# Count stage of a sparse attention kernel: first spreads moved ahead of the branch, projections spread over all counting rounds, query bias added by TensorE, mask kept as 0/1

## The reference, cut to what matters

```python
idx = prior_indices[:Ss]                     # 1024 queries x 32 keys, all key numbers under 256
Q, K, V = (proj(Wq, bq), proj(Wk, bk), proj(Wv, bv))   # x @ W.T + b, 2 batches, 16 heads of 16
s_scores = jnp.einsum('bhsd,bhskd->bhsk', Q, K[:, :, idx]) * scale
s_scores = jnp.where(prior_index_mask, s_scores, -inf)
sparse_out = jnp.einsum('bhsk,bhskd->bhsd', softmax(s_scores), V[:, :, idx])
...
out = sparse_out @ Wo.T + bo                 # if lam >= 1 for the batch, else a dense attention
x = x + ffn0(out)                            # a dense two-layer network
x = x + experts(cond1(x))                    # a second network, 8 experts, the best 2
```

## Time and profile before

| | |
|---|---|
| median of 3 runs | 575.02 us (574.04 to 575.03) |
| the profiled execution, its own time | 575.06 us |
| its span in the trace | 573.0 us |
| TensorE (PE) busy | 523.4 us, 91% of the span |
| VectorE (DVE) busy | 407.1 us, 71% |
| ScalarE (ACT) busy | 225.8 us, 39% |
| GpSimd (POOL) busy | 84.2 us, 15% |
| HBM | 26 GB/s over the span |

### The profile page before, as it was taken

The page is one execution under the profiler, slowest core; times in us unless marked ns, Lnnn a source line. Parts: engine busy times, 40 slices in busy tenths (PEclk is TensorE's granted clock), DMA queues, the critical chain, the costliest instruction groups (busy, mean ns, idle before and its releaser), DMA issues.

```text
span 573.0 us, 7404 instructions
## 1 busy us (share of the span) xinstructions
PE 523.4 (91%) x2649; PEld 361.9 (63%) x2649; DVE 407.1 (71%) x788; ACT 225.8 (39%) x381; POOL 84.2 (15%) x94
## 2 busy tenths in 40 slices
PE   3897788999899999989779999999999999999897
PEld 1454354454454454435557887888878888788786
DVE  5887879969896878734666588483884838848286
ACT  4204376667566576664345250032500325003100
POOL 3002643315123121200131100010000100000000
PEclk9998899999999999989879999999999999999989
DMA  6100010101010000000252000100001000010000
GB/s 248 56 2 1 0 38 37 38 1 38 1 37 1 1 0 2 3 0 1 80 146 73 1 2 18 47 9 0 2 19 46 11 0 2 18 47 0 11 9 27
DMA packets 11757, 15.38 MB, mean 27 GB/s; under 512 B 5954, under 2 KB 8258, under 8 KB 11714
## 3 DMA queue, kind: packets, MB, share of 16 engines
q1 hardware_dynamic: 11714, 14.83, 8.1%
HBM read 12.73 MB, written 2.10 MB: 26 GB/s over the span
## 4 chain that ended last, share of the span: by engine, by line
PE 72%; DVE 13%; ACT 8%; issue 3%; POOL 2%; DMA 1%; SPq 0%; ACTq 0%; DVEq 0%; POOLq 0%
PE psS L524 6%; PE psO L540 5%; PE psG L1544 4%; PE psG L1546 4%; PE psG L1545 4%; PE psM L1544 3%; PE psM L1546 3%; PE psM L1545 3%; PE psO L1544 3%; PE psO L1545 3%; PE psO L1546 3%; PE psG L504 3%; PE psS L1544 3%; PE psG L506 3%; PE psS L1546 3%
## 5 line engine op out<-in xcount | busy, mean ns | idle before, releaser
L737 DVE TENSOR_REDUCE few_Qa<-psG 128x2 fp32r<-128x512 f32 x116 | 74.6, 686 | 29.6 <-PE psG L506 29.5
L657 ACT ACTIVATE Pr<-psS 128x512 f32<-128x512 f32 x128 | 71.5, 599 | 30.1 <-PE psS L528 21.1
L744 DVE SCALAR_TENSOR_TENSOR Pr<-Pr,few_W 128x1024 f32<-128x1024 f32 x48 | 72.8, 1519 | 11.8 <-ACT Pr L657 11.6
L524 PE MATMUL psS<-few_QAT,few_KP 128*128 128x512 f32 x128 | 53.2, 460 | 10.5 <-ACT Pr L657 9.8
L504 PE MATMUL psG<-few_KG,QG 128*128 128x512 f32 x116 | 52.3, 508 | 3.7 <-DVE few_Qa L737 3.7
L1654 ACT ACTIVATE V<-psS,cols 128x512 f32<-128x512 f32 x16 | 11.0, 691 | 103.7 <-PE psS L1546 103.0
L524 PEld LDWEIGHTS psS<-few_QAT,few_KP 128*128 128x128 f32 x128 | 22.6, 190 | 39.1 <-issue 31.5
L506 PE MATMUL psG<-Mneg,few_identb 128*128 128x512 bf16 x116 | 46.2, 398 | 0.0
L1693 DVE TENSOR_TENSOR hT_lo<-V,hT_hi 128x512 fp32r<-128x512 f32 x64 | 44.3, 692 | 2.2
L1691 DVE CAST hT_hi<-V 128x512 fp32r<-128x512 f32 x64 | 36.3, 567 | 12.5 <-ACT V L1654 6.7
L540 PE MATMUL psO<-Pr,few_VA 128*17 128x512 f32 x256 | 34.4, 612 | 0.0
(11 more groups left out here) (251 smaller groups left out, 1196.9 us busy)
## 6 DMA issues: line engine op xcount, KB each, us to landing
Pr<-xT_dram SPq DMA_DIRECT2D x2, 1024.0 KB, 8.3
staged<-w_dram SPq DMA_DIRECT2D x4, 512.0 KB, 3.6
x1T<-xT_dram SPq DMA_DIRECT2D x4, 512.0 KB, 4.2
staged<-ew_dram SPq DMA_DIRECT2D x4, 512.0 KB, 3.9
out_dram<-y SPq DMA_DIRECT2D x16, 128.0 KB, 1.7
staged<-fc_dram SPq DMA_DIRECT2D x2, 512.0 KB, 4.0
Pr<-wqkv_dram SPq DMA_DIRECT2D x1, 768.0 KB, 4.8
staged<-fc2a_dram SPq DMA_DIRECT2D x1, 512.0 KB, 4.7
```

What stands on the lines that cost most here:

```text
L524: mm = nc.tensor.matmul(psS[:, f, :], self.KP[:, u % 2, j, r * P:r * P + P], self.QAT[:, u % 2, j // 2, q], start=True, stop=not logged)
L657: nc.scalar.activation(Pr[:, i % JOBS, 512 * f:512 * f + 512], psS[:, f, :], ACT.Exp, scale=SCALE).then_inc(self.s["s_exp"], 1)
L737: nc.vector.tensor_reduce(self.Qa[:, f % SLOTS, st, 2 * p:2 * p + 2, 48], self.guard_bank(i)[0][:, p, :].rearrange("p (h t) -> p h t", h=2 ...
L744: nc.vector.scalar_tensor_tensor(pr, pr, FMAX, self.W[:, r, :], ALU.min, ALU.mult).then_inc(self.s["s_prob"], 1)
```

## The change

- The spreads of rounds 0 and 1 are issued ahead of the branch, by the setup code; all spreads now use psO alone, so each waits for ScalarE's copy of the one before it. The general form of the attention waits for these two copies. The transpose of the flag's maximum goes to psG and stands between the two spreads; the f16 identity is made ahead of the maximum.
- The projections use the two banks of psM alone and are spread over the halves 2 to 14 by the table PROJECTED_AFTER. Each waits for the copy of the one two before it.
- The query bias is split into two fp32r parts, and TensorE adds each with one matmul (a row of ones, 1x128, times the bias, 1x256) to each of the 16 query tiles. ScalarE copies the tile to Qn (before, VectorE's L688 added the bias). Keys and values are still added by VectorE, two halves later than they were projected.
- GpSimd makes the low part of the bias ahead of clearing its buffers; for that it waits for ScalarE's copy of the high part (bias_hi), which stands behind the branch and four constants.
- The counts of half 0 are copied by ScalarE, those of half 1 by VectorE. The second transpose of the counts goes to psM, so that it needn't wait for the mask of the first. The mask is 0 or 1 and the identity that it is multiplied with (few_identn) is -1e30; its first part is made by ScalarE, its second by VectorE.
- The logarithm takes the counts plus 2^-100 directly, and the marks of empty counts are made from it by ScalarE (a second pass of Relu, 128x2048); VectorE has one pass of it left.

The core of the diff:

```diff
-PROJ_FROM = 3
-ADD_AFTER = (1, 2, 4, 5, 7)
+PROJECTED_AFTER = (0, 0, 1, 1, 2, 1, 2, 1, 2, 1, 1, 2, 2, 2, 2, 0)
+ADD_LATER = 2
...
         def setup_tensor(pe):
+            pe.wait_ge(s["consts_ready"], 1)
+            pe.wait_ge(s["idx_ready"], 1)
+            few_keys.spread_tensor(pe, 0)
             pe.wait_ge(s["greatest"], 1)
             pe.wait_ge(L["cst"], 16)
-            nc.tensor.transpose(psM[0:1, 0, 0:P], flags[:, 0:1], ident).then_inc(s["greatest_full"], 1)
+            nc.tensor.transpose(psG[0:1, 0, 0:P], flags[:, 0:1], ident).then_inc(s["greatest_full"], 1)
+            few_keys.spread_tensor(pe, 1)
...
+                eng.wait_ge(few_keys.s["bc_out"], 2)
...
+            for k in range(2):
+                few_keys.spread_act(act, k)
...
-                for k in range(2):
-                    yield "spread", k
-                for k in range(STEPS):
-                    for j in (2 * k + 2, 2 * k + 3):
-                        if j < STEPS:
-                            yield "spread", j
-                    if PROJ_FROM <= k < STEPS - 1:
-                        for j in range(len(ADD_AFTER)):
-                            yield "project", (k - PROJ_FROM) * len(ADD_AFTER) + j
-                    if k == STEPS - 1:
+                tiles = list(self.projected_tiles())
+                n, adds = 0, {}
+                for e in range(STEPS * NT):
+                    if e % NT == 0 and e // NT + 2 < STEPS:
+                        yield "spread", e // NT + 2
+                    yield "count", e
+                    for m in adds.pop(e, ()):
+                        yield "add", m
+                    for m in range(n, n + PROJECTED_AFTER[e]):
+                        yield "project", m
+                        if not tiles[m][0]:
+                            adds.setdefault(e + ADD_LATER, []).append(m)
+                    n += PROJECTED_AFTER[e]
+                    if e == STEPS * NT - 2:
                         yield "guard_keys", 0
                         yield "fill", 0
-                    yield "count", k
                 yield "counted", 0
+                yield "counted", 1
...
+            def spread_tensor(self, pe, i):
+                if i:
+                    pe.wait_ge(self.s["bc_out"], i)
+                flat = psO[:, :, :].rearrange("p a b -> p (a b)")
+                for qq in range(4):
+                    for j in range(4):
+                        p0 = i * 16 + qq * 4 + j
+                        mm = nc.tensor.matmul(flat[32 * j:32 * j + 32, qq * 256:qq * 256 + 256],
+                                              ident16[:, p0:p0 + 1].to_broadcast([P, 32]),
+                                              idxm[:, :], start=True, stop=True, tile_position=(0, 32 * j))
+                mm.then_inc(self.s["bc_full"], 1)
+            def spread_act(self, act, i):
+                act.wait_ge(self.s["bc_full"], i + 1)
+                nc.scalar.copy(self.idxb[:, i, :],
+                               psO[:, :, :].rearrange("p a b -> p (a b)")).then_inc(self.s["bc_out"], 1)
...
             def pool(self, pool):
+                nc.gpsimd.memset(self.one[:, :].bitcast(F32), 1.0).then_inc(self.s["ones"], 1)
+                nc.gpsimd.memset(self.tiny[:, 0:1], 2.0 ** -100).then_inc(self.s["tiny"], 1)
+                nc.gpsimd.memset(self.tiny[:, 1:2], -1.0).then_inc(self.s["tiny"], 1)
+                pool.wait_ge(self.s["bias_hi"], 1)
+                nc.gpsimd.tensor_tensor(self.bq[:, 1, :], bqkv[0:1, 0:D], self.bq[:, 0, :].bitcast(F32),
+                                        ALU.subtract).then_inc(self.s["bias_lo"], 1)
                 nc.gpsimd.memset(self.Qa[:, :, :, :, :].bitcast(F32), 0.0).then_inc(self.s["cleared"], 1)
...
+                pe.wait_ge(self.s["consts"], 4)
...
+                        if i >= 2:
+                            pe.wait_ge(self.s["q_out" if tiles[i - 2][0] else "va_out"], self.of_kind(i - 2))
...
-                            mm = nc.tensor.matmul(PROJ[i % 4][:, 0:w1 - w0], xT[:, kk, b * S + tt * P:b * S + tt * P + P],
-                                                  wqkv[:, kk, w0:w1], start=(kk == 0), stop=(kk == KD - 1))
+                            mm = nc.tensor.matmul(psM[:, i % 2, 0:w1 - w0], xT[:, kk, b * S + tt * P:b * S + tt * P + P],
+                                                  wqkv[:, kk, w0:w1], start=(kk == 0), stop=(kk == KD - 1 and not is_q))
+                        if is_q:
+                            if self.of_kind(i) == 1:
+                                pe.wait_ge(self.s["ones"], 1)
+                                pe.wait_ge(self.s["bias_lo"], 1)
+                            for part in (1, 0):
+                                mm = nc.tensor.matmul(psM[:, i % 2, 0:D], self.one[:, :], self.bq[:, part, :],
+                                                      start=False, stop=(part == 0))
...
+                        pe.wait_ge(self.s["w0_out"], 1)
+                        pe.wait_ge(self.s["w1_out"], 1)
+                        pe.wait_ge(self.s["bc_out"], STEPS)
                         if i:
-                            pe.wait_ge(self.s["neg_out"], i)
-                        flat = psO[:, :, :].rearrange("p a b -> p (a b)")
+                            n = at["neg1_out", 0]
+                            for name, j in order[n - 3:n - 1]:
+                                pe.wait_ge(self.s[name], j + 1)
+                        flat = (psM if i else psO)[:, :, :].rearrange("p a b -> p (a b)")
...
+                nc.scalar.mul(self.identn[:, :], ident, -BIG).then_inc(self.s["consts"], 1)
+                act.wait_ge(L["bqkv"], 16)
+                nc.scalar.copy(self.bq[:, 0, :], bqkv[0:1, 0:D]).then_inc(self.s["bias_hi"], 1)
+                tiles = list(self.projected_tiles())
                 for what, i in [*self.opening(), *self.due()]:
                     u = i // JOBS
                     if what == "spread":
-                        act.wait_ge(self.s["bc_full"], i + 1)
-                        nc.scalar.copy(self.idxb[:, i, :],
-                                       self.spread_bank(i)[:, :, :].rearrange("p a b -> p (a b)")).then_inc(self.s["bc_out"], 1)
-                    if what == "counted":
-                        for tt in range(NT):
-                            act.wait_ge(self.s["eq_used"], STEPS * NT - NT + 1 + tt)
-                            bank = psS if tt else psG
-                            nc.scalar.copy(self.W[:, tt, :], bank[:, :, :].rearrange("p a b -> p (a b)")).then_inc(self.s["w_out"], 1)
+                        self.spread_act(act, i)
...
+                    if what == "project" and tiles[i][0]:
...
+                        nc.scalar.copy(q, psM[:, i % 2, 0:D].rearrange("p (g e) -> p g e", e=P)).then_inc(self.s["q_out"], 1)
+                    if what == "counted" and i == 0:
+                        act.wait_ge(self.s["eq_used"], STEPS * NT - 1)
+                        nc.scalar.copy(self.W[:, 0, :], psG[:, :, :].rearrange("p a b -> p (a b)")).then_inc(self.s["w0_out"], 1)
...
+                    if what == "turn_counts" and i == 0:
+                        act.wait_ge(self.s["turned_full"], 1)
+                        nc.scalar.activation(Mneg[:, 0:S], psO[:, :, :].rearrange("p a b -> p (a b)"), ACT.Relu,
+                                             bias=1.0, scale=-1.0).then_inc(self.s["neg0_out"], 1)
                     if what == "logs":
-                        act.wait_ge(self.s["atleast1"], 1)
-                        nc.scalar.activation(self.logs, self.marks, ACT.Ln).then_inc(self.s["ln_out"], 1)
+                        act.wait_ge(self.s["tiny"], 2)
+                        act.wait_ge(self.s["w1_out"], 1)
+                        nc.scalar.activation(self.logs, self.W[:, :, :], ACT.Ln, bias=self.tiny[:, 0:1]).then_inc(self.s["ln_out"], 1)
+                        act.wait_ge(self.s["ln_out"], 1)
+                        nc.scalar.activation(self.none, self.logs, ACT.Relu, bias=self.tiny[:, 1:2],
+                                             scale=-1.0).then_inc(self.s["none_out"], 1)
...
+                    if what == "add":
+                        dve.wait_ge(self.s["proj_full"], i + 1)
                         if i == 0:
...
+                    if what == "counted" and i == 1:
+                        dve.wait_ge(self.s["eq_used"], STEPS * NT)
+                        nc.vector.tensor_copy(self.W[:, 1, :], psS[:, :, :].rearrange("p a b -> p (a b)")).then_inc(self.s["w1_out"], 1)
+                    if what == "turn_counts" and i == 1:
+                        dve.wait_ge(self.s["turned_full"], 2)
+                        nc.vector.tensor_scalar(Mneg[:, S:2 * S], psM[:, :, :].rearrange("p a b -> p (a b)"),
+                                                0.0, None, ALU.is_equal).then_inc(self.s["neg1_out"], 1)
...
+                        dve.wait_ge(self.s["none_out"], 1)
```

(1 more changed line is left out.)

137 lines of the change are left out of this document (57 added, 80 removed).

## The result

The changed kernel takes 590.36 us (median; 589.10 to 591.53) where the kernel before takes 575.02 us: the ratio is 1.0277, with an interval of 1.0258 to 1.0297. It is slower, by more than the forecast of 580.0 us and outside the range of 575.0 to 582.8 us. The profiled execution took 589.31 us, its span is 587.5 us against 573.0 us. The four runs differ with the mean granted clock: 589.10 and 589.31 us at 0.983, 591.40 and 591.53 us at 0.973 and 0.971.

What follows compares the result with a forecast made beforehand. VectorE was taken to bound the opening until 21 us, TensorE until 48.2 us, then a serial piece. Terms 4.0 - 0.8 + 1.7 = +4.9 us on 575.06 us gave 580.0 us, range 575.0 to 582.8 us.

Steps and rivals of the forecast that it cites:

- the collision with the clears: GpSimd's clears, about 11.0 to 16.15 us, hold up VectorE's comparisons: 3.3 us; rival that they do not, chance 0.28.
- the slow start of the dense phase: TensorE at 1.2 GHz for the first 2.8 us of its dense phase: 1.4 us lost.
- the serial end: First query transpose to E: copies of counts -0.8 us, then mask, table load, logarithm and last pass +1.7 us.
- the term for the 32 bias matmuls: TensorE's dense phase: 0.12 us for each bias matmul, 3.85 us in all; rival that they cost nothing, chance 0.10.
- everything behind E is shifted by as much: Behind E, order and sizes are the same in both programs, so a shift of E shifts the end equally.
- E: End of VectorE's last pass of the logarithm, 60.4 us before; forecast 4.9 us later, at about 65.3 us.
- The start: Work up to the sum of half 2: spreads, branch, constants, first comparisons and clears; that sum ready at 16.9 us.
- The dense phase: TensorE from the sum of half 2 to the last projection: 29.7 us old work, 3.85 us bias, 1.4 us clock.
- weight loads bind: Rival for the bias matmuls: 0.20 us each, 2.6 us more, 582.6 us in all; chance 0.12.
- The rule on weight loads: For one-row bias matmuls: loads go by columns, not rows, estimated 107 ns each, 3.4 us in sum.
- The clock: TensorE at half speed after near idleness from 13.5 to 16.9 us, for 2.8 us: 1.4 us lost.
- the dearest case: Upper end of the range: each bias matmul costs its weight load of 0.20 us, 582.6 us; chance 0.12.

Runs made afterwards that it cites:

- e2: Changed kernel with GpSimd's clears of few_Qa and few_Ka ahead of the branch, few_KP's behind the first low parts of queries: 585.63 us, ratio 1.0215.
- e1: Changed kernel without its 32 bias matmuls, which leaves the query bias out of the result: 582.21 us, ratio 1.0161.
- e3: Changed kernel with the bias matmuls over all 128 rows (1/128 times the bias on every partition) instead of one row: 585.91 us, ratio 1.0226.
- e5: e4 with one bias matmul per query tile in place of two, high part in rows 0 to 63, low part in 64 to 127: 578.78 us, ratio 1.0077.
- e6: e5 with ScalarE's logarithm and Relu pass ahead of its half of the mask: 575.86 us, ratio 1.0031.
- g1: Kernel before with clears ahead of the branch and the change's end of the opening, logarithm ahead of ScalarE's mask: 574.73 us, ratio 1.0009.
- g2: Kernel before with clears and the first two spreads ahead of the branch, still in two banks: 571.57 us, ratio 0.9955.
- g3: Kernel before with clears and two spreads ahead of the branch and the new end, logarithm first: 574.85 us, ratio 1.0012.
- h2: Kernel before with one unused buffer of 32 bytes in each partition among the attention's: 576.00 us, ratio 1.0028.
- e4: Changed kernel with the edits of e2 and e3 together: 579.20 us, ratio 1.0096.
- h1: Changed kernel with few_tiny 64 bytes in place of 32 in each partition, which moves Wo, w1 and w2: 589.72 us, ratio 1.0272.
- h5: Changed kernel with 32 more bytes in the unused gap right ahead of Wo, w1 and w2: 588.73 us, ratio 1.0256.
- e7: e6 without bias matmuls, VectorE adding the query bias as in the kernel before: 573.28 us, ratio 0.9978.
- f1: Kernel before with clears of few_Qa and few_Ka ahead of the branch, few_KP's behind the first low parts of queries: 571.81 us, ratio 0.9961.

## Why the prediction was wrong

**The direction held, and so did the collision with the clears, the slow start of the dense phase and the serial end. What failed is the term for the 32 bias matmuls, and with it the assumption that everything behind E is shifted by as much.** By the prediction's own steps:

- *The start.* Sum of half 2 forecast at 16.9 us, measured 17.81 us. The chain of steps ahead of the branch was right within 0.3 us for the spreads and their copies (5.54, 6.61, 7.70 us) and about 1 us too late for TensorE's third spread (9.49 us in place of 10.5). The mis-sized part is the clears: I let a comparison through at the end of each, as the earlier trace rows has it. With GpSimd busy from 9.80 to 15.41 us none came through: the seventh comparison was held for the whole time, 5.76 us in place of 0.48 us, and with it half 1 already. e2 confirms the place; the size is 4.5 us at the sum of half 2, where 3.3 us were forecast.
- *The dense phase.* From the sum of half 2 to the end of the last projection I had 29.7 + 3.85 + 1.4 = 34.95 us, it took about 42.1 us. **This is the step that failed: the term of 3.85 us for the 32 bias matmuls.** They cost 8.3 us (e1). The term was 0.12 us for each, "near the transposes, whose loads follow each other in this rhythm". That is what they do cost with 128 rows (e3, e5: 0.12 and 0.13 us); but the transposes are of full size and these aren't, and the one-row form adds 4.5 us (e3), because the loads of the pair and of the projection behind it aren't hidden. The rival "weight loads bind" saw the load of the bias matmul at 0.20 us and missed the one of the projection behind it. Another 1.7 us are 9 times 0.19 us: the last tile ahead of a sum or a spread takes 1.06 us even without the bias (e1), and I had priced all 16 tiles at half of 1.73 us, the figure within a row of tiles. The tiles of keys and values, 1.91 us each, are 0.8 us over my figure: I had taken the drain between two out of the earlier trace rows, but with a sum of counts between them it isn't hidden.
- *The rule on weight loads.* By "TensorE: Matmul & The Clock Gate" of the Trainium skill, "LDWEIGHTS (loading the stationary operand)", the load goes by columns, and the trace agrees: a load of one row takes 0.18 us and one of 128 rows 0.19 us. The estimate of 107 ns is too low for both. But that the load stands in nobody's shadow made it dear here, and that isn't in the estimate of 3.4 us.
- *The clock.* 1.4 us forecast; the first tile (3.18 us in place of 1.91) and the sum ahead of it (1.00 us in place of 0.55) lost 1.7 us. The size was right in part by luck: I took the clock to fall after a rise, as in the kernel before, and 2.8 us of low clock; it had not risen at all by then and stayed low for the first 3.6 us, until 21.38 us.
- *The serial end.* -0.8 + 1.7 = +0.9 us forecast. From first transpose to E it is 13.1 us after and 12.2 us before: right, also by its parts (-1.0 us up to both copies of counts, +1.9 us from there). e6 gives the order of ScalarE's passes 1.7 us, and g1 has the new end in the better order as dear as the old one.
- *Everything behind E is shifted by as much.* This fell by 1.4 us in the profiles (13.1 us at E, 14.5 us at the end), and I had given it no rival. The profile of before has 1.5 us of low clock at 249 us that the other hasn't, so 2.9 us are to be found behind 271 us. The pace of the matmuls with the moved weights is a large part: 48 with Wo, 192 with w1 and 192 with w2, each 6.3 ns slower, are at most 2.7 us, and between the profiles of g2 and g3, where E is the same, the distance grows by 2.3 us. The measured times give 1.6 us in h2. A second wait of TensorE of 1.39 us, three matmuls behind the join of the two branches, is there in the changed kernel, in e2, e3, e4, h1 and h5 (1.2 to 2.2 us), and in no other; what makes it stays open. These are the six kernels with 32 bias matmuls.

The chances were 0.78 for slower, which it was. The range ended at 582.8 us because the dearest case had one load for each bias matmul and nothing behind E.

The parts of the change come out as follows. The spreads ahead of the branch are harmless and worth at most 0.5 us of E. The projections spread over all rounds bring no earlier end of the projections, but let VectorE finish its comparisons 6 us sooner, which is worth 1.1 us of E together with the spreads and the new end (e7 against f1). The bias on TensorE costs 8.3 us of E in its one-row form. The 0/1 mask and the short logarithm, made to take work off VectorE, bring nothing by themselves (g1). The best version is the kernel before with the clears ahead of the branch, with or without the two spreads: 0.9961 (0.9946 to 0.9975) and 0.9955 (0.9940 to 0.9971).

## What to carry to other kernels

Price a one-row matmul between full ones with its own load and that of the next one too, and not by its columns; if it has to be there, fill its rows (here with 1/128 in each). Large clears on GpSimd belong where VectorE has nothing to do, and their worst case is one comparison that waits for all of them. Before a printed clock of 1.00 is believed, compare the pace of equal matmuls in both stretches. When a change allocates even 32 bytes, compare the pace of the same matmuls far behind it in both traces before the time is put down to the change itself.

## What the runs showed of the hardware

- A projection of 128 rows behind a one-row matmul takes 1.06 us in the chain, behind a full one 0.87 us; the one-row pair 0.43 us, a full pair 0.24 us. So the form with 1/128 of the data is the dearer one, by 4.5 us for 16 pairs.
- Three clears of 2.65, 0.52 and 1.80 us in a row let none of VectorE's comparisons through; the one that had begun ahead of them ended after the last. "SBUF — State Buffer" of the Trainium skill, "SBUF: two separate sides", speaks of a lock and not of shared bandwidth; the trace agrees (a comparison of 5.76 us in place of 0.48).
- The pace of TensorE was about half of the later one up to 21.38 us in the changed kernel (spreads of 1.07 us in place of 0.61 us) and up to 12.61 us in e2. The granted clock has its first record there; the 1.00 that is printed ahead of it stands for no record.
- Matmuls of 128x512 follow each other at 0.227 or 0.233 us by where in a partition their weights start. 32 unused bytes cost this kernel 0.28% of its time (0.12% to 0.44%).
